# A two-layer graph transformer on one core: the row maxima turned in float32r onto q in PSUM, their splitting spread, and the attention sums copied at a step's head

## The reference

```
def layer(x, adj, ...):
    qkv = layer_norm(x, g1, be1) @ w_qkv
    q, k, v = split into 8 heads of 16
    scores = einsum('nhd,mhd->hnm', q, k) * HEAD_DIM ** -0.5
    scores = where(adj != 0, scores, -inf)
    attn = softmax(scores, axis=-1)
    out = einsum('hnm,mhd->nhd', attn, v)
    x = x + out @ w_proj + b_proj
    h2 = layer_norm(x, g2, be2)
    return x + gelu(h2 @ w1 + b1) @ w2 + b2
```

## Time and profile before

| | |
|---|---|
| median of 3 runs | 3741.22 us (3737.74 to 3742.95) |
| profiled execution, its own time | 3741.04 us |
| its span | 3739.3 us |
| mean granted PE clock | 0.944 |
| PE busy | 3467.5 us (93%) |
| DVE busy | 2969.6 us (79%) |
| ACT busy | 2334.8 us (62%) |
| POOL busy | 2489.5 us (67%) |

### The profile page before, as it was taken

The page is one execution under the profiler, slowest core; times in us unless marked ns, Lnnn a source line. Parts: engine busy times, 40 slices in busy tenths (PEclk is TensorE's granted clock), DMA queues, the critical chain, the costliest instruction groups (busy, mean ns, idle before and its releaser), DMA issues.

```text
span 3739.3 us, 68583 instructions
## 1 busy us (share of the span) xinstructions
PE 3467.5 (93%) x22572; PEld 1404.7 (38%) x22572; DVE 2969.6 (79%) x8997; ACT 2334.8 (62%) x2596; POOL 2489.5 (67%) x1476
## 2 busy tenths in 40 slices
PE   6999999999999999997678999999999999999976
PEld 3443333333333333333434433333333333333234
DVE  6889898888888898841368999999999999999323
ACT  5358686868687777764241466666666666666732
POOL 1067877787878787885010578887878888878930
PEclk9589999999999999998896799999999999999988
DMA  4578787878787878662132546464646565545421
GB/s 137 169 238 259 244 260 236 257 232 263 222 278 221 278 224 281 215 195 76 57 104 87 176 136 190 140 192 139 187 142 183 146 187 147 180 148 175 117 65 51
DMA packets 480351, 676.31 MB, mean 181 GB/s; under 512 B 51552, under 2 KB 272864, under 8 KB 475616
## 3 DMA queue, kind: packets, MB, share of 16 engines
q1 hardware_dynamic: 479568, 671.83, 58.1%
q10 hardware_dynamic: 432, 0.10, 0.0%
HBM read 508.14 MB, written 165.68 MB: 180 GB/s over the span
## 4 chain that ended last, share of the span: by engine, by line
PE 39%; POOL 35%; issue 15%; DVE 7%; DMA 2%; POOLq 1%; ACT 1%; DVEq 0%; SPq 0%; ACTq 0%
POOL arena L921 35%; PE PS L464 12%; PE PS L444 9%; PE PS L477 7%; PE PS L471 6%; DVE spill L798 5%; PE PS L417 3%; POOLq L899 1%; PE PS L450 1%; DVE arena L758 0%; DVE neg_hi L806 0%; DMA arena<-out_dram 0%; PE PS L408 0%; ACT o_sb L673 0%; DMA mask<-in_adj_t 0%
## 5 line engine op out<-in xcount | busy, mean ns | idle before, releaser
L798 DVE CUSTOM_DVE_ANT_0 spill<-PS,mask_n 128x512 bf16<-128x512 f32 x4096 | 2635.8, 688 | 282.2 <-PE PS L444 182.3
L921 POOL TENSOR_TENSOR arena<-arena,mask 128x1024 int32<-128x1024 int32 x896 | 2137.8, 2386 | 646.4 <-ACT arena L665 641.3
L665 ACT ACTIVATE arena<-PS 128x1024 f32<-128x1024 f32 x2048 | 1991.3, 1022 | 919.0 <-PE PS L477 876.4
L444 PE MATMUL PS<-k_t,q_t 48*128 48x512 f32 x4096 | 1287.7, 546 | 61.7 <-DVE pmax L798 41.5
L464 PE MATMUL PS<-arena,v_sb 128*32 128x512 f32 x8192 | 1105.0, 612 | 41.7 <-ACT o_sb L673 37.6
L444 PEld LDWEIGHTS PS<-k_t,q_t 48*128 48x128 f32 x4096 | 546.4, 194 | 1028.8 <-DVE pmax L798 910.9
L471 PE MATMUL PS<-q_t,k_t 50*128 50x512 f32 x4096 | 931.6, 464 | 0.5 <-POOL arena L911 0.4
L477 PE MATMUL PS<-arena,idb 64*128 64x512 bf16 x4312 | 840.9, 390 | 0.0
L471 PEld LDWEIGHTS PS<-q_t,k_t 50*128 50x128 f32 x4096 | 400.2, 188 | 201.9 <-ACT arena L665 123.9
L477 PEld LDWEIGHTS PS<-arena,idb 64*128 64x128 bf16 x4312 | 209.0, 95 | 462.8 <-issue 337.9
L798 DVE DVE_READ_ACCUMULATOR2_ANT pmax<- 128x1 f32 x4096 | 340.1, 83 | 0.0
(11 more groups left out here) (54 smaller groups left out, 970.7 us busy)
## 6 DMA issues: line engine op xcount, KB each, us to landing
mask<-m_dram SPq DMA_DIRECT2D x768, 256.0 KB, 2.7
mask_n<-mn_dram SPq DMA_DIRECT2D x768, 128.0 KB, 2.7
adj_in<-in_adj SPq DMA_DIRECT2D x256, 256.0 KB, 3.8
mask<-in_adj_t SPq DMA_DIRECT2D x256, 256.0 KB, 4.0
m_dram<-mask SPq DMA_DIRECT2D x256, 256.0 KB, 3.7
mn_dram<-mask_n SPq DMA_DIRECT2D x256, 128.0 KB, 3.8
mt_dram<-arena SPq DMA_DIRECT2D x256, 128.0 KB, 3.5
arena<-mt_dram SPq DMA_DIRECT2D x256, 128.0 KB, 2.8
```

Of the source, the lines that this page charges most:

```text
L444: pe.matmul(bank, q_t[r0:r0 + KROWS, gb % Q_SLOTS, pair, q * P:(q + 1) * P], k_t[r0:r0 + KROWS, pair, mb * TILE:(mb + 1) * TILE], start=Tr ...
L665: nc.scalar.activation(p_buf[:, t % P_SLOTS, 2 * half:2 * half + 2, :], ps_b[:, 2 * half:2 * half + 2, :], ACT.Exp, scale=SCALE).then_inc( ...
L798: dve.tensor_tensor_reduce(spill[:, j % A_BANKS, :], ps_a[:, j % A_BANKS, :], mask_n[:, v % N_SLOTS, :], 1.0, LOWEST, ALU.subtract, ALU.ma ...
L921: pool.tensor_tensor(p, p, m, ALU.mult).then_inc(p_masked, 1)
```

## The change

Five things are changed.

1. **The turn.** A turn job is now one product of a float32r identity (`idr`, new) with the pair's `q_t` rows (128 x 512), and then four products of `stage` with `idr` (128 x 128 each) that add to it in the same bank, all in float32r. ACT's new `keep_q` copies the bank onto `q_t`. DVE's `add_neg` is gone. A bank that held a turn job becomes free by `q_ready` of ACT.
2. **The splitting.** `split_neg` with its drains is gone. `reduce_max`, `round_neg` (which writes the rounded value straight to `stage`) and `rest_of_neg` stand behind the first, second and third `take_max` of the next pass.
3. **The order of jobs.** Every step has four score jobs; the turn jobs are added as fifth jobs to steps 29 and 30 of the pass before.
4. **keep_o** stands ahead of both halves of the exponent of step 2, where it stood between them.
5. SP's order of loads follows the new numbering of visits; its loads are the same.

```diff
+for _t in range(-(FIRST // 4), STEPS):
+    for _n in range(scores_before(_t), scores_before(_t + 1)):
+        SCORE_JOB.append(len(JOBS))
+        JOBS.append(("score", _n))
+    if (_t + 3) % MT < 2 and -3 <= _t < STEPS - 3:
+        TURNS.append(_t)
+        JOBS.append(("turn", len(TURNS) - 1))
...
             def a_job(L, j):
...
-                    for t in range(NS):
-                        mm = pe.transpose(bank[:, t * P:(t + 1) * P], stage[:, t * 2 + i % 2, :], idf[:])
-                    mm.then_inc(a_scored, 1)
+                    pe.wait_ge(neg_ready, L * PASSES + p + 1)
+                    pe.matmul(bank, idr[:], q_t[:, (L * NB + p // 2) % Q_SLOTS, p % 2 * 2 + n % 2, :],
+                              start=True, stop=False)
                     for t in range(NS):
+                        mm = pe.matmul(bank[:, t * P:(t + 1) * P], stage[:, t * 2 + n % 2, :], idr[:],
+                                       start=False, stop=t == NS - 1)
+                    mm.then_inc(turned, 1)
...
                 if s == 0:
-                    pe.wait_ge(a_done, L * NJ + JOB_AT["turn", nb, 2 * quad + 1] + 1)
+                    pe.wait_ge(q_ready, L * 2 * PASSES + 2 * (t // MT) + 2)
...
+            def keep_q(L, n):
+                act.wait_ge(turned, L * 2 * PASSES + n + 1)
+                j = JOBS.index(("turn", n))
+                nc.scalar.activation(q_t[:, (L * NB + n // 4) % Q_SLOTS, n % 4, :], ps_a[:, j % A_BANKS, :],
+                                     ACT.Copy).then_inc(q_ready, 1)
...
                 for t in range(STEPS):
-                    exp_pair(L, t, 0)
                     if t > LAG and t % MT == LAG:
                         keep_o(L, t // MT - 1)
+                    exp_pair(L, t, 0)
                     exp_pair(L, t, 1)
+                    if t in TURNS:
+                        keep_q(L, TURNS.index(t))
...
-            def add_neg(L, j):
-                _, p, _, _, pair = JOBS[j]
-                dve.wait_ge(a_scored, L * NJ + j + 1)
-                rows = q_t[:, (L * NB + p // 2) % Q_SLOTS, pair, :]
-                dve.tensor_tensor(rows, ps_a[:, j % A_BANKS, :], rows.bitcast(F32), ALU.add).then_inc(a_done, 1)
+            def reduce_max(L, p):
+                dve.wait_ge(a_done, L * NSC + (p + 1) * UNITS)
+                dve.tensor_reduce(neg[:], pmax[:, p % 2], AXIS.X, ALU.max, negate=True).then_inc(neg_reduced, 1)
+
+            def round_neg(L, p):
+                dve.wait_ge(neg_reduced, L * PASSES + p + 1)
+                dve.wait_ge(turned, (L * PASSES + p) * 2)
+                dve.tensor_copy(hi, neg4).then_inc(neg_rounded, 1)
+
+            def rest_of_neg(L, p):
+                dve.wait_ge(neg_rounded, L * PASSES + p + 1)
+                dve.tensor_tensor(lo, neg4, hi.bitcast(F32), ALU.subtract).then_inc(neg_ready, 1)
```

More of the change, by code:

```diff
@@ L351, in _ @@
                 for nb in range(NB):
-                    order.append((step_of_job(JOB_AT["score", 2 * nb, 0, 0, 0]) - 12, "q", nb))
+                    order.append((step_of_score(2 * nb * UNITS) - 12, "q", nb))
                 for i in range(2 * NB):
@@ L483, in b_step @@
                 nb, quad, s = t // (2 * MT), t // MT % 2, t % MT
-                jobs = range(jobs_before(t), jobs_before(t + 1))
+                jobs = STEP_JOBS[t]
                 for j in jobs[:2]:
@@ L815, in add_neg @@
[L815 to L828 removed]
+            rows = stage[:].rearrange("p g (a c) -> p g a c", a=2)
@@ new lines, in _ @@
+            hi, lo = rows[:, :, :, KROWS:KROWS + 1], rows[:, :, :, KROWS + 1:KROWS + 2]
+            neg4 = neg[:].rearrange("p (g a c) -> p g a c", a=2, c=1)
+            def reduce_max(L, p):
[5 more added lines that the diff above has]
+                dve.tensor_copy(hi, neg4).then_inc(neg_rounded, 1)
```

112 lines of the change are left out of this document (52 added, 60 removed).

## The result

| | before | after |
|---|---|---|
| median of the runs | 3739.48 us (3737.36 to 3742.95, 4 runs) | 3795.49 us (3788.54 to 3801.8, 4 runs) |
| ratio after / before, 95% | | 1.0148 [1.0129, 1.0168] |
| profiled execution, its own time | 3741.04 us | 3801.8 us |
| its span | 3739.3 us | 3800.0 us |
| mean granted PE clock | 0.944 | 0.934 |

The changed kernel is slower by 56 us; 3753 was forecast, with a range up to 3790. The profiled execution is the slowest of the four, 6 us over their median.

A forecast was written before the change was run, and what follows sets the result against it. PE and DVE, both nearly full in the middle of a pass, were taken as the bound. Heads -73, turns +74, first-layer even passes +10, last turns +2, pipeline fill -1 gave +12 on 3741.0: 3753 us, range 3698 to 3790.

The forecast's parts named there:

- Heads together: Steps 0 to 2 of each pass: four jobs and the earlier keep_o save 77, less 4 for mask rows, 73 us.
- Steps 0 and 1: Head of a pass: with four score jobs they become normal-length steps, 1.22 us saved in 15 passes a layer, 36.6.
- the splitting decides the sign: Turn: spread over three maxima, rounding and subtraction each wait for POOL, ending at 3.33 and 6.07 us; 21 turns cost +74.
- Forecast 7.0 over five steps: Steps 27 to 31: 5.8 us over normal steps plus 1.2 for clock, against 3.48 before, in 21 turns.
- With 0.15 for the change of operands, it is 1.05, twice a turn: Each turn job on PE: 0.9 us, from bounds 0.48 to 1.15, plus 0.15 for changing operands.
- the 1.2 taken: Turn: half PE clock expected after nearly every one, costing 1.2 us instead of 1.61.
- The even passes of the first layer: Their 7 turns: the subtraction waits for a short POOL piece at most, 1.4 us a turn, +10.
- N: Length of one step in the middle of a pass before the change, 2.767 us.
- B: Rival at the turn: no wait for POOL, a turn 2.7 us over five steps, no slow clock; 3653 us, chance 0.12.
- C: Rival at the turn: the rounding waits for POOL, the subtraction does not; 3703 us, chance 0.10.
- D: Rival at the turn: dearer 128-column products (+15) and half clock for twice as long (+25); 3793 us, chance 0.08.
- E: Rival at the turn: PE's clock holds, so the 1.2 us in 21 turns falls away; 3728 us, chance 0.10.

The follow-up runs named there:

- e8: The kernel before with only keep_o moved ahead of both exponents of step 2; 3695.36 us, ratio 0.9884 to before.
- e5: e3 with DVE's wait for a visit's mask placed two maxima earlier, ahead of the third maximum of the visit before; 3622.82 us, 0.9689 to before.
- e2: e1 with reduction, rounding and subtraction together behind the first maximum; 3762.88 us, 1.0064 to before.
- e3: e1 with the splitting made of reductions alone, at the same places between the maxima; 3673.51 us, 0.9817 to before.
- e9: e5 with the subtraction again a two-operand operation, the rounding still a reduction; 3637.42 us, 0.9718 to before.
- e10: e5 with the rounding again a copy, the subtraction still a reduction; 3663.07 us, 0.9786 to before.
- e7: e3 with every score job two places earlier, so steps start with a visit's third job, the mask wait untouched; 3627.87 us, 0.9704 to before.
- e4: e1 with a useless 640-column reduction added on DVE in step 0 of 15 passes a layer; 3801.56 us, 1.0162 to before.
- e1: The changed kernel with the identity's rounding moved behind the memsets at program start; 3797.21 us, 1.0147 to before.

## Why the prediction was right about the turn and wrong about the step

**Right in sum, in part by luck: the heads.** "Heads together: 77 - 4 = 73 saved" was measured as 73.4 in after. The parts were 36.5 for keep_o and 36.6 for steps 0 and 1. e8 shows 41.3 for keep_o, without the very first head: the mask rows took less back than the 4 us forecast, and two heads had also lost clock to its wait. Steps 0 and 1 gave less: from e8 to after a head falls from 9.52 to 8.46, 1.06 instead of 1.22, because the new steps are 2.82 long, and in the last pass of a layer, which has no score jobs, nothing. That is some 30 us. The two misses cancel. In the second layer steps 0 to 2 are of the longer kind, 136.0 us of heads against 134.3 in e5, where they are not.

**Right: the splitting decides the sign.** The forecast had the rounding done at 3.33 and the subtraction at 6.07 us after the start of step 28, each at the end of a POOL masking; in after it is 3.09 and 5.90, each at the end of a masking. e2, e3, e9 and e10 show that this is the cause: with the same jobs in the same order DVE does not wait for POOL when both are reductions (e3, e5), waits once when they stand together (e2), and the whole price comes only with both of the old kind and apart. The Trainium skill's rule on the port shared by VectorE and GpSimd (SBUF — State Buffer, "SBUF: two separate sides"), by which the subtraction should wait as the rounding does, holds in these rows: 1.03 us and 2.29 us. Reductions in their place took 0.18 us.

**Right in sum, off in its parts: the turn.** Forecast 7.0 over five steps, measured 7.42 in the second layer. Over the 21 turns the tails rose by 81 us instead of 74. "With 0.15 for the change of operands, it is 1.05, twice a turn": a turn job at full clock is 0.82, and of the four 128-column products two gaps in three are about 0.11 and one 0.06, near the lower of the bounds of 0.06 and 0.23. Against that, the clock cost more than the 1.2 taken: 0.84 or 0.78 in eight of the fourteen windows. The even passes of the first layer cost 0.4 a turn, 3 us, instead of the 1.4 and 10 us taken; the subtraction there met no long masking (0.18 us).

**The step that failed: "Steps 0 and 1 get four jobs. They become N steps."** N was read from before, 2.767 us, and taken as a property of a step with four score jobs. It is not: it is that of a step that begins with a visit's third job. The fifth jobs in steps 0 and 1 looked like 1.22 us a pass to be saved, and they were also what put the mask wait where DVE has slack. With them gone, each of the 24 middle steps took 0.056 us more: +37.0 in the middles, which the sum had at nothing, and which is most of the 49 us between 3753 and the profiled 3801.8. e5 (the wait moved) and e7 (only the jobs moved) both bring N back to 2.767, and e4 shows that a late DVE hides the longer step for three steps and no more. The sign was there to read: steps 29 to 31 of the very pass of the earlier trace rows took 2.82 with four score jobs each.

**Left out: the identity's rounding.** The prediction costed what the change adds to the passes, and not the one instruction that it adds at the start. There it stands ahead of the memsets and waits for a DMA; +6 us in the trace, gone with e1, though the times don't resolve it. With it the first step comes 7.2 us later, where the forecast had 1 us saved.

Of the rivals, B and C are out for this kernel: the rounding waited, and so did the subtraction. B gave 3653 for a kernel without the waits: e3 took 3673.5 with the longer step, e5 3622.8 without it, 30 us less than B. B put a turn at 2.7 over five steps; e5 shows 15.70 - 13.84 = 1.86. D, 3793, was nearest to the measured time, by luck: its dearer products were not there, its longer half clock was there in part (8 of 14 windows), and the 37 us of the middles are not in it. E asked for the clock to hold; it fell in all fourteen turns of after and in none of e3's and e5's, which have the same turn jobs. So here the clock goes with PE's waiting for DVE and not with the turn jobs; why in before it fell in nine turns of fourteen with nearly the same wait, no run shows.

## What to carry to other kernels

- Before you spread small operations over an engine's work, ask of each whether it waits for another engine. Two that do can share one wait when they stand together (e2, 34 us less than e1); apart, each finds a new one (+14.6 or +40.3 us where only one waits, +116.9 where both do). Better is a form that doesn't wait: here a reduction over an axis of length one or two in place of a copy and a subtraction.
- A steady step's length belongs to its alignment too. When a change shifts which job of a group falls at a step's head, look for instructions that only some jobs have, a second wait above all, before you take the old step for the new one. Look also for the new alignment in the old trace: three steps of each pass had it here, and their length (2.82) was the forecast's missing number.
- A setup instruction that waits for a load goes behind the setup work that doesn't. And an edit with several parts is worth trying in parts: keep_o alone (e8) gives 1.2%, and the whole change with another splitting and the mask wait moved (e5) gives 3.1%, where the change as it was lost 1.5%.

## What was not expected of the hardware

- An extra wait on DVE that is already fulfilled costs about 0.1 us (0.64 instead of 0.54 from product to maximum) where the start is on the path. Two maxima further on it leaves the step at 2.767; whether it is quite free there, no run without it shows.
- A reduction rounds to float32r on its way out, from 16 to 16 columns, in 0.18 us beside a running POOL instruction, where the rounding copy of the same values took up to 2.38.
- Float32r products of 128 columns with 128 stationary columns come 0.06 to 0.11 us apart at full clock, no slower than the float32 transposes of before (0.11).
